# Attention's row scores half a group further ahead, and the row maximum turned in the middle of a group

## The reference

```python
def heads(W):
    return (x @ W).reshape(B, S, NUM_HEADS, D_K).transpose(0, 2, 1, 3)
Q, K, V = (heads(WQ), heads(WK), heads(WV))
score = jnp.einsum('bhqd,bhkd->bhqk', Q, K) / jnp.sqrt(jnp.asarray(D_K, x.dtype))
score = score + mask                     # -inf above the diagonal
score = score - jnp.max(score, axis=-1, keepdims=True)
score = jnp.exp(score)
score = score / jnp.sum(score, axis=-1, keepdims=True)
out = jnp.einsum('bhqk,bhkd->bhqd', score, V)
...
x = x + _L0_attn_ref(_layernorm(x), ...)
x = x + _L0_ffn_ref(_layernorm(x), ...)      # 8 experts, top 2, fixed capacity
x = x + _L1_attn_ref(_layernorm(x), ...)     # a gated linear recurrence and an FFN
x = x + _L1_ffn_ref(_layernorm(x), ...)
```

## Time and profile before

| | |
|---|---|
| median of 3 runs | 701.99 us (700.9 to 704.29) |
| the profiled execution | 706.4 us, its span 704.7 us |
| PE busy | 580.7 us, 82% of the span |
| DVE busy | 428.0 us, 61% |
| ACT busy | 301.6 us, 43% |
| POOL busy | 167.7 us, 24% |
| mean granted TensorE clock | 0.932 of full speed |
| attention's 16 groups | about 44 to 250 us of the span |

### The profile page before, as it was taken

One profiled execution on the slowest core, in us unless ns is written; L12 is line 12 of the kernel. 1 busy time (PEld: TensorE's weight loads), 2 busy tenths in 40 slices (PEclk: granted clock), 3 DMA queues, 4 the chain that ended last, 5 costly groups with the idle time before them and its releaser, 6 DMA issues.

```text
span 704.7 us, 9209 instructions
## 1 busy us (share of the span) xinstructions
PE 580.7 (82%) x3296; PEld 435.8 (62%) x3296; DVE 428.0 (61%) x1072; ACT 301.6 (43%) x435; POOL 167.7 (24%) x184
## 2 busy tenths in 40 slices
PE   2488989898889751999960868889999999998997
PEld 1445556555556431778750647668887888787876
DVE  6676778868878642143324696599467956764241
ACT  3225555444545410344420532385256625662361
POOL 3001212342252344000005744350230023001100
PEclk9999999999999955899995888899999999999999
DMA  3314222123210033475411100000000000000000
GB/s 106 120 47 172 75 102 86 43 79 112 73 56 24 9 112 105 147 235 152 116 38 31 30 15 16 1 23 9 0 1 17 1 0 1 16 1 0 1 16 15
DMA packets 40910, 38.83 MB, mean 55 GB/s; under 512 B 3104, under 2 KB 31776, under 8 KB 40864
## 3 DMA queue, kind: packets, MB, share of 16 engines
q1 hardware_dynamic: 38816, 34.04, 15.4%
q0 software_dynamic: 2048, 4.20, 1.9%
HBM read 23.54 MB, written 14.68 MB: 54 GB/s over the span
## 4 chain that ended last, share of the span: by engine, by line
PE 62%; DVE 14%; issue 9%; POOL 7%; ACT 6%; DMA 1%; DVEq 0%; POOLq 0%; ACTq 0%
PE ps L1852 6%; PE ps L1805 5%; PE ps L1814 5%; PE ps L1874 5%; PE ps L1588 5%; PE ps L1875 4%; PE ps L1559 4%; PE ps L1955 4%; PE ps L1951 4%; PE ps L1952 4%; PE ps L1878 4%; PE ps L1576 3%; DVE pm L966 3%; POOL xs_dram L496 3%; POOL PT L510 2%
## 5 line engine op out<-in xcount | busy, mean ns | idle before, releaser
L637 ACT ACTIVATE PT<-ps 128x768 f32<-128x768 f32 (+1 forms) x96 | 84.6, 883 | 82.5 <-PE ps L1576 81.3
L966 DVE TENSOR_REDUCE pm<-ps 128x4 f32<-128x512 f32 x160 | 104.3, 686 | 23.6 <-PE ps L1562 10.8
L510 POOL TENSOR_SCALAR_AFFINE_SELECT PT<-PT 128x512 f32<-128x512 f32 x64 | 40.1, 638 | 164.1 <-ACT PT L637 163.2
L1559 PE MATMUL ps<-KP,QS 128*128 128x512 f32 x160 | 67.8, 452 | 7.6 <-DVE pm L966 5.9
L1576 PE MATMUL ps<-QM,KP 128*128 128x512 f32 (+3 forms) x256 | 62.2, 346 | 0.5 <-DVE QM L980 0.4
L1588 PE MATMUL ps<-PT,V 128*32 128x128 f32 (+3 forms) x512 | 46.2, 455 | 14.1 <-POOL PT L510 14.1
L1559 PEld LDWEIGHTS ps<-KP,QS 128*128 128x128 f32 x160 | 29.2, 192 | 36.7 <-DVE pm L966 34.7
L727 ACT ACTIVATE HT<-ps,cols 128x640 f32<-128x640 f32 x32 | 25.4, 795 | 58.2 <-PE ps L1805 58.2
L1576 PEld LDWEIGHTS ps<-QM,KP 128*128 128x128 f32 x256 | 40.6, 195 | 9.0 <-issue 4.0
L1359 DVE TENSOR_TENSOR_SCAN zero<-decay,OG 128x512 f32<-128x512 f32 x32 | 42.2, 1318 | 1.1
L1814 PE MATMUL ps<-W,HT 128*128 128x128 f32 x320 | 37.9, 278 | 3.2 <-ACT HT L727 3.2
(11 more groups left out here) (289 smaller groups left out, 1308.5 us busy)
## 6 DMA issues: line engine op xcount, KB each, us to landing
qk_dram<-HL SPq DMA_DIRECT2D x8, 512.0 KB, 3.2
W<-in_eW SPq DMA_DIRECT2D x16, 256.0 KB, 3.3
QS<-qk_dram SPq DMA_DIRECT2D x64, 48.0 KB
KP<-qk_dram SPq DMA_DIRECT2D x64, 48.0 KB
xs_dram<-zero SPq DMA_DIRECT2D x4, 640.0 KB, 5.3
XS<-xs_dram SPq DMA_DIRECT2D x8, 320.0 KB, 4.7
ys_dram<-zero SPq DMA_DIRECT2D x8, 320.0 KB, 2.9
qk_dram<-HL SPq DMA_DIRECT2D x8, 256.0 KB, 3.4
```

Of the source, the lines that this page charges most:

```text
L510: g.affine_select(out=diag, in_=diag, pattern=[[0, 4], [1, P]], compare_op=ALU.is_ge, fill=0.0, base=0, channel_multiplier=-1).then_inc(se ...
L637: act.activation(PT[:, 2 * i:2 * i + 2, a:z], ps[:, 2 * (n % 2) + 2:2 * (n % 2) + 4, 0:z - a], ACT.Exp, scale=float(DK) ** -0.5).then_inc( ...
L966: v.tensor_reduce(pm[:, t, k, :], bank[n % 2].rearrange("p (i n) -> p i n", n=P), AXX, ALU.max).then_inc(pair_free[n % 2], 1)
L1559: mm = pe.matmul(to, QS[:, G % 2, t * P:(t + 1) * P], KP[:, G % 3, k, :, :].rearrange("p i n -> p (i n)"), start=True, stop=t != k)
```

## The change

The row scores of a group are made half a group earlier. Before, group w held all ten units of group w+1. Now it holds units 5 to 9 of w+1 in its first half and units 0 to 4 of w+2 in its second half. The merge of the maxima of w+1, its turning and `add_max` move from the end of group w to its middle; on DVE `add_max` now stands behind the first two reductions of group w+2. The work of the tails is put at other places in the group, on PE, DVE and ACT. The numbers of the ring and of the turns follow. SP's code and POOL's code are as before, but what they wait for comes at other times. No instruction is added or removed.

```diff
 def _ring():
...
+    for u in range(10):
+        at[u, 0] = len(at)
+    for u in range(AHEAD):
+        at[u, 1] = len(at)
+    for w in range(NW):
+        for u in range(AHEAD, 10):
+            if w + 1 < NW:
+                at[u, w + 1] = len(at)
...
+        for u in range(AHEAD):
+            if w + 2 < NW:
+                at[u, w + 2] = len(at)
...
@@ ACT
                 exp_unit(w, 0)
-                if b and g == 2:
-                    take_turn("turn2", b - 1, xn2T[:, :])
                 if b and g == 3:
                     gate_exp(b - 1)
+                exp_unit(w, 1)
                 if w:
                     store_sums(w - 1)
                 if g == 0 and b:
                     split_v(b)
-                exp_unit(w, 1)
+                if b and g == 2:
+                    take_turn("turn2", b - 1, xn2T[:, :])
                 exp_unit(w, 2)
...
@@ DVE
             minus_max(0)
+            row_max(1, 0)
+            row_max(1, 1)
             add_max(0)
+            for n in range(2, AHEAD):
+                row_max(1, n)
...
                 if rows_next:
-                    row_max(w + 1, 0)
-                    row_max(w + 1, 1)
+                    for m in range(AHEAD, 9):
+                        row_max(w + 1, m)
                 if b and g == 1:
                     add()
                 if b and g == 3:
                     ranks()
                 if rows_next:
-                    row_max(w + 1, 2)
-                    row_max(w + 1, 3)
+                    row_max(w + 1, 9)
+                if g == 0 and b + 1 < NB:
+                    make_halves(b + 1)
+                if rows_next:
+                    minus_max(w + 1)
+                if w:
+                    normalise(w - 1)
                 if b and g == 1:
                     stats_()
                 if b and g == 3:
                     place()
+                if w + 2 < NW:
+                    row_max(w + 2, 0)
+                    row_max(w + 2, 1)
                 if rows_next:
...
+                    add_max(w + 1)
+                if w + 2 < NW:
+                    row_max(w + 2, 2)
+                    row_max(w + 2, 3)
                 if b and g == 1:
                     norm()
+                if w + 2 < NW:
+                    row_max(w + 2, 4)
                 if b and g == 2:
                     take_logits()
...
                     choose()
@@ PE
                 key_scores(w, 0)
+                rows(w + 1, 5, 6)
+                key_scores(w, 1)
+                rows(w + 1, 7, 8)
+                if w:
+                    values(w - 1, 2)
+                    values(w - 1, 3)
                 if b and g == 1:
                     times_wo(b - 1)
                 if b and g == 2:
                     turn_normed(b - 1)
                 if b and g == 3:
                     ranks(b - 1)
...
+                rows(w + 1, 9)
+                key_scores(w, 2)
+                if g == 0 and b + 1 < NB:
+                    project(b + 1)
                 if w:
                     turn_out(w - 1)
...
                 values(w, 0)
...
+                rows(w + 2, 0, 1)
                 key_scores(w, 3)
...
+                if w + 1 < NW:
+                    turn_max(w + 1)
+                rows(w + 2, 2, 3)
+                key_scores(w, 4)
+                rows(w + 2, 4)
+                values(w, 1)
                 if b and g == 0:
                     turn_heads(b - 1)
                 if b and g == 2:
                     logits(b - 1)
```

More of the change, by code:

```diff
@@ L1667, in _, with rows @@
             turn_max(0)
+            for u in range(AHEAD):
+                row_scores(1, u)
             for w in range(NW):
                 b, g = w // NG, w % NG
[L1670 to L1673 removed]
+                def rows(group, *units):
+                    if group < NW:
+                        for u in units:
+                            row_scores(group, u)
                 key_scores(w, 0)
+                rows(w + 1, 5, 6)
[4 more added lines that the diff above has]
+                    values(w - 1, 3)
                 if b and g == 1:
@@ L1708, in _ @@
                     logits(b - 1)
-                key_scores(w, 4)
-                values(w, 1)
-                if rows_next:
-                    turn_max(w + 1)
                 key_scores(w, 5)
```

54 lines of the change are left out of this document (7 added, 47 removed).

## The result

The changed kernel takes 725.6 us (median of 4 runs, 723.98 to 725.7), the kernel before in the same job 702.98 (4 runs). The ratio is 1.0319, 95% interval 1.0287 to 1.0352: slower by 22.6 us. The forecast was 713 and its range ended at 722, so the sign was right and the size was not. The profiled execution took 725.7 us, 19.3 more than that of before.

What follows compares the result with a forecast made beforehand. It took PE and DVE, leading in turn in a ring through add_max, as the bound, neither full. Group changes summed to +11.4 us, mostly from load waits, taking the median from 702.0 to 713, range 702 to 722.

Steps and rivals of the forecast that it cites:

- The sum: All attention groups: lengthenings and savings add up to +11.4 us, profiled execution from 706.4 to 718.
- the lower clock: Rival, PE in three more groups: standing behind place and statistics lowers the granted clock; +5, 718 us; chance 0.17.
- The load ring: Row scores, two reductions, add_max, QS and KP loads, next row scores: 12.0 us a plain group, against 11.2 before.
- The landing: KP loads on SP: first issue to landed taken as 6.4 us, between bounds of 5.8 and 7.7.
- second leg: SP's KP load after the last key scores: free about when the QS issues end, so it adds nothing.
- This is the term that decides: Loads of QS and KP, gated by add_max: they set plain groups at 12.0 us, against 10.9 for the other work.
- Without any load a plain group would be 10.9: Plain groups: first half 5.9 and second half 5.0 us, only 0.3 under before.
- the no-ring case: Rival: landing is short enough or waits fall where PE waits anyway; +5.3 us instead of 11.4, 707; chance 0.17.
- Groups with g = 3: Groups 7 and 11: choose spills in, DVE does reductions, ranks, merge, division and place; 15.7 us each.
- the order of POOL's scatters stands as before: 0: Group 15: scatter order on POOL unchanged, so no change in time, 0 us.
- Groups with g = 1: Groups 5, 9 and 13: DVE waits for the output projection and computes statistics; 14.1 us each.
- Faster: Rival, DVE: the turned maximum no longer stops it; up to 13.2 us go, two thirds give 693; chance 0.11.

Runs made afterwards that it cites:

- E5: Changed kernel with POOL's clearing of the second chunk ahead of the first three scatters in groups 7, 11 and 15; 724.9 us.
- E3: Changed kernel with three QS slots and four KP slots, so both load gates are open; 725.2 us.
- E9: Kernel before the change with three QS slots and four KP slots, as a control; 707.3 us, ratio 1.0075.
- E1: Changed kernel with a third QS slot, so the QS load waits for an older add_max; 727.0 us.
- E2: Changed kernel with a fourth KP slot, so the KP load waits for older key scores; 730.3 us.
- E4: Changed kernel with turn_max two steps earlier on PE and add_max ahead of the first two reductions on DVE; 726.5 us.
- E10: Changed kernel with three QS and four KP slots, and row scores spread one by one on PE instead of in pairs; 715.5 us.
- E7: Changed kernel with three QS and four KP slots, and each row reduction over half of the keys; 707.9 us.
- E8: Kernel before the change with each row reduction over half of the keys; 688.1 us.
- E11: Changed kernel with DVE's place steps ahead of minus_max and normalise in groups 7 and 11; 719.1 us.
- E13: Changed kernel with three QS and four KP slots (the fourth set up by POOL), row scores spread on PE, place ahead of minus_max; 705.9 us, ratio 1.0052.
- E12: Changed kernel with its own two QS and three KP slots, and row scores spread one by one on PE; 720.9 us.

## Why the prediction was wrong

Point by point, in the profiled executions; the working is the prediction's.

**The sum.** Forecast +11.4, measured +20.1 up to the end of group 15, of which 0.9 come back behind it.

| groups | forecast | measured |
|---|---|---|
| 0, with its start | +1.6 | 60.59 - 59.45 = +1.1 |
| 1 to 3 | +2.3 | 37.49 - 33.68 = +3.8 |
| 4 | +0.2 | 14.34 - 14.12 = +0.2 |
| 5 to 8 | +2.0 | 59.31 - 54.91 = +4.4 |
| 9 to 12 | +4.6 | 58.64 - 50.44 = +8.2 |
| 13, 14 | +0.7 | 24.71 - 23.87 = +0.8 |
| 15 | 0 | 14.00 - 12.48 = +1.5 |

**The steps that failed in the sum.** It is 8.7 us short. Groups 7 and 11 have 3.8 of it (15.7 forecast for each), groups 8 to 10 have 2.0, group 15, which was put at 0, has 1.5, and groups 1 to 3 have 1.5; the rest about cancels. The largest missing term is the clock: the sum has none, and the lower clock stands among the rivals with a chance of 0.17, though the earlier trace rows showed it in group 7. Its size can only be estimated. By PE's busy time, group 8 has 14.46 us against 13.40 in group 4, group 9 has 13.49 against 12.23 in group 5, group 10 has 12.47 against 12.18 in group 6, group 12 has 12.42 against 11.42 in E5 at the full clock, and group 11 has 14.02 against the 11.35 of before, of which I leave 0.5 to the new order. That makes some 5 to 6 us. The rival's own price, +5, was about right; the mistake was to set it beside the forecast and not into it.

**The load ring: right in mechanism, too short by a term, and given too much of the cause.** The landing was taken as 6.4, nearer to the lower bound, and was about 7, so that plain groups came to 12.5 and not 12.0: +1.5 over three groups. The Trainium skill's 2.0 us (DMA: Bandwidth & Descriptors, Anatomy of one DMA), from which the prediction worked out an estimate of 4.9, are stated there for the DMAs that GpSimd issues; these loads are issued by SP, and measured about 7. E3 with its control E9 prices the whole ring at 4.6 us. E1, E2 and E4 show its second leg, the last key scores, which stands beside the first: in the changed kernel they end at 73.45, and the last `QS` issue at 73.65. That leg could have been read from the code and the 0.2 us between the two times.

**The step that failed in the mechanism** is "This is the term that decides", said of the load, and with it the sentence "Without any load a plain group would be 10.9", with its like for groups 6 and 12 (12.3 and 11.3), from which the no-ring case got its 707. Without the loads (E3) a plain group is 11.3, group 6 12.7 and group 12 13.0, and the kernel stands 18 us above its control, not 5. I had added DVE's chain up as if PE could hand it a row score at any time. In the new order seven row scores, 2 to 8, stand close together on PE with two banks between them. E10 shows what spreading them gives back: 9.8 us once the loads are out of the way, the clock's part included. That the distance on the two banks is the whole reason is not shown, since halved reductions (E7 against E8) leave 0.6 to 0.8 us in the groups with tails. In group 6 of before, the tail's matmuls had filled the hole in which PE waits for `add_max`, and the group was full at 11.29; in the changed order there was no such hole, so the tail's work came on top.

**Groups with g = 3** were put at 15.7 and took 17.3 and 17.9. Up to the end of `add_max` the walk holds: 12.8 and 13.6 us into groups 7 and 11 (213.31 - 199.70 for the latter), against 13.2 forecast. From there 2.5 became 4.5 and 4.3. Part of this is the clock, since the values took 1.51 us in both groups instead of 0.85; part are the waits, of 0.3 us for a reduction and 0.7 and 0.6 for the clearing. I had priced `place` as work that DVE does, and left out who waits for its result: POOL's scatters, with the clearing behind them, for which PE waits. I had also written that in group 15 "the order of POOL's scatters stands as before: 0". The order stood, but what they wait for moved, since `place` now follows `normalise`: +1.5, of which E11 gives back 1.4 (12.6).

**Groups with g = 1** were put at 14.1 and took 13.6 at the full clock (groups 5 and 13): DVE's chain was overrated there by 0.5.

**The clock** was a rival, not a term. It came together with the forecast, not in its place. Group 8 took 15.24 at a clock of 0.89, group 4 with like work 14.34 at 1.00; group 9 took 14.89 at 0.91, group 5 13.64. That is 2.2 us in these two, beside what it costs in groups 10, 11 and 12; in group 7 it was 0.90 before as well. E5 and E11 support that the waits of groups 7 and 11 pull it down behind them: where scatters and clearing come in another order or earlier, groups 8 and 12 run at 0.99 to 1.00 in both traces, at 0.89 and 0.85 in the changed kernel. Group 9 doesn't prove it. The clock also falls there, and in group 5, without any edit that bears on it. E11 and the changed kernel are the same program up to group 6, and group 5 took 13.64 us at 1.00 in the one and in E11:
```profile
112.89:127.84 14.95, 13.54 (x81) 7.71 (x80) 11.09 (x33) 5.96 (x8) 3.46 (x5) 0.90 0.10 31
```
So 1.3 us of a single group can be chance between two executions.

**The other rivals.** "Faster" said that the wait of 13.2 us for the turned maximum might be the whole price. The wait did vanish, and brought nothing in the changed kernel, where PE is held in the same group by the load, the reductions or its own work. Only with the loads and the pairs of row scores out of the way (E10, E13) do plain groups gain, 0.6 us each.

**What stays open.** The longer PE time in the new order, 0.5 us in group 6 (E7 and E8), is measured, not explained. Of E11's 6.5 us the groups with `place` and group 15 account for 4.3; the rest is within what the starts and the clock of single profiled executions differ by. That the clock fell because PE stood still is only argued. The medians differ by 22.6 us and the two profiled executions by 19.3, since that of before was 3.4 us above its median; no trace shows this part.

## What to carry to other kernels

When work is moved ahead across a ring buffer, list every gate of the loads that it needs, not the one that seems last: here two stood 0.2 us apart, and opening either bought nothing. When two engines pass a few banks back and forth, look at the distance between two users of the same bank, and not only at the sum of either's work: spreading out ten units of row scores gave back 4.7 us by itself and 9.8 with the loads out of the way, where removing the load ring was worth some 4.6. When busy time grows with no work added, look at the clock first, and put it into the sum. And a stall that a fuller group used to fill isn't free to remove: the work that sat in it has to go somewhere.

## What the runs showed of the hardware

The granted clock also fell in plain groups without any tail. In E12, PE in group 2 and a stretch behind it:
```profile
82.20 0.47 PE L1578 MATMUL ps<-KP,QS 128*128 128x512 f32 x1 [2.02 <-DMA KP<-qk_dram]
```
```profile
84.00:86.00 2.00, 2.00 (x11) 1.90 (x9) 1.75 (x3) 0.04 (x1) 0.63 (x1) 0.50 0.00 0
```
After 2.0 us of standing still the clock was 0.50 (1.2 GHz) and the group took 14.3 us with 12.2 of busy PE, where its neighbour with the same work took 11.6 with 10.7. The waits for the load of the changed kernel in groups 1 to 3, 0.9 to 1.4 us each, left it at 1.00. A late load can so cost more than its lateness. In group 5 of E11 (shown above) the clock was 0.90 without a wait of such length, which I can't explain.

Four loads of 24 rows, issued 0.73 us apart, took some 7 us from the first issue to the release of the matmul (73.70 to 80.80), in a kernel whose DMA was a quarter busy in that stretch.
